# A two-layer recurrence on one core: a loop body of four slots, and two copies by ScalarE

## The reference

```python
xW = jnp.einsum('ntd,dh->nth', x, Wx) + b
def step(h_prev, xw_t):
    h_next = jnp.tanh(h_prev @ Wh + xw_t)
    return (h_next, h_next)
x = x + _L0_cond_ref(x, cond_1024, L0_cond_Wx, L0_cond_Wh, L0_cond_b)
x = x + _L1_cond_ref(x, cond_1024, L1_cond_Wx, L1_cond_Wh, L1_cond_b)
```

## Time and profile before

| what | before |
|---|---|
| median of three runs | 2059.51 us |
| profiled execution, first to last instruction | 2057.6 us |
| TensorE matmul / weight load busy | 2044.6 / 1863.8 us |
| VectorE busy | 1746.3 us |
| ScalarE busy | 1280.9 us |
| GpSimd busy | 444.9 us |
| one slot in the steady part | 1.98 us |

### The profile page before, as it was taken

How to read it: one execution, slowest core, us unless ns; L and a number is a source line. 1 busy time by engine, 2 the same in 40 slices (tenths; PEclk the granted TensorE clock), 3 DMA queues, 4 the chain that set the end, 5 groups by cost and what they waited for, 6 DMA issues and landing times.

```text
span 2057.6 us, 219078 instructions
## 1 busy us (share of the span) xinstructions
PE 2044.6 (99%) x98388; PEld 1863.8 (91%) x98388; DVE 1746.3 (85%) x10221; ACT 1280.9 (62%) x6660; POOL 444.9 (22%) x2054
## 2 busy tenths in 40 slices
PE   8999999999999999999999999999999999999999
PEld 6999999999999999999999999999999999999997
DVE  5888888888888888888888888888888888888887
ACT  4666666666666666666666666666666666666665
POOL 3222222222222222222222222222222222222221
DMA  3000000000000000000000000000000000000000
GB/s 108 25 26 25 26 25 26 25 26 25 27 24 27 24 28 24 28 24 28 24 27 24 27 24 27 24 27 24 28 23 28 23 27 24 27 24 27 24 27 15
DMA packets 111960, 56.33 MB, mean 27 GB/s; under 512 B 12432, under 2 KB 111008, under 8 KB 111520
## 3 DMA queue, kind: packets, MB, share of 16 engines
q1 hardware_dynamic: 111168, 53.53, 8.8%
q10 hardware_dynamic: 576, 1.18, 0.2%
q0 software_dynamic: 32, 0.02, 0.0%
HBM read 37.90 MB, written 16.78 MB: 27 GB/s over the span
## 4 chain that ended last, share of the span: by engine, by line
PE 99%; DMA 1%; issue 0%; DVE 0%; ACT 0%; SPq 0%; ACTq 0%
PE ps_rec L270 44%; PE ps_rec L287 33%; PE ps_xw L247 22%; DMA wx<-wx_in 0%; DMA wh<-wh_in 0%; PE ps_rec L339 0%; DVE zt L463 0%; ACT h L387 0%; SPq L223 0%; ACTq L421 0%; ACTq L420 0%; DVE z L472 0%; DVE x_out L503 0%; SPq L222 0%
## 5 line engine op out<-in xcount | busy, mean ns | idle before, releaser
L270 PE MATMUL ps_rec<-wh,h 128*32 128x128 f32 x33024 | 1261.2, 273 | 3.3 <-ACT h L387 2.8
L387 ACT ACTIVATE h<-z 128x24 f32<-128x24 f32 x4066 | 654.7, 208 | 666.4 <-DVE z L472 625.0
L287 PE MATMUL ps_rec<-wh_part,h 128*32 128x128 bf16 x48792 | 1036.9, 219 | 1.5 <-issue 1.5
L270 PEld LDWEIGHTS ps_rec<-wh,h 128*32 128x32 f32 x33024 | 880.0, 109 | 30.1 <-ACT h L387 6.7
L287 PEld LDWEIGHTS ps_rec<-wh_part,h 128*32 128x32 bf16 x48792 | 724.0, 96 | 151.1 <-issue 1.8
L205 POOL TENSOR_TENSOR h<-h 128x16 f32<-128x16 f32 x2032 | 430.6, 212 | 1589.9 <-DVE h L205 1589.9
L472 DVE TENSOR_REDUCE z<-zt 128x24 f32<-128x72 f32 x4066 | 664.5, 205 | 69.7 <-DVE zt L463 0.6
L376 ACT ACTIVATE ps_rec<-ps_xw,mask 128x128 f32<-128x128 f32 x2048 | 664.2, 324 | 77.9 <-PE ps_xw L247 77.9
L463 DVE STREAM_TRANSPOSE zt<-ps_rec 128x128 f32<-128x128 f32 (+1 forms) x2063 | 649.8, 316 | 18.7 <-PE ps_rec L270 12.7
L205 DVE TENSOR_TENSOR h<-h 128x16 f32<-128x16 f32 x2034 | 356.0, 175 | 209.2 <-ACT h L387 0.2
L247 PE MATMUL ps_xw<-wx,x_pe 128*32 128x128 f32 x8248 | 404.6, 273 | 2.0 <-issue 1.1
(11 more groups left out here) (20 smaller groups left out, 16.5 us busy)
## 6 DMA issues: line engine op xcount, KB each, us to landing
x_pe<-x_t SPq DMA_DIRECT2D x256, 64.0 KB, 2.0
x_dve<-x_t SPq DMA_DIRECT2D x256, 64.0 KB, 1.9
out_t<-x_out SPq DMA_DIRECT2D x256, 64.0 KB, 1.5
wh<-wh_in SPq DMA_DIRECT2D x1, 1024.0 KB, 5.7
wx<-wx_in SPq DMA_DIRECT2D x1, 1024.0 KB, 8.3
wx<-wx_in ACTq DMA_DIRECT2D x1, 512.0 KB, 5.2
wx<-wx_in SPq DMA_DIRECT2D x1, 512.0 KB, 5.0
wh<-wh_in SPq DMA_DIRECT2D x1, 512.0 KB, 7.2
```

Source lines behind the costliest of these rows:

```text
L270: mm = pe.matmul(rows(ps_rec[l][n % 2], g), h_step(l, n - 1)[:, k, :], wh[l][:, k, g * P:(g + 1) * P], start=False, stop=k == KC - 1 and n ...
L287: mm = pe.matmul(rows(ps_rec[l][n % 2], g), h_bits(l, n - 1)[:, k, :], wh_part[l][:, i, at:at + P], start=False, stop=k == KB[l] - 1 and i ...
L387: act.activation(h_of(l, n)[:, tiles, :], src[:, tiles, :], ACT.Tanh).then_inc(h_count(l, n)[0], 1)
```

## The change

- `RING` becomes 4: h is kept for four steps instead of eight, and TensorE's loop body has four slots (254 turns instead of 127). LAG stays 7. Counts that were lowered every four slots are lowered every two (`PAIR`).
- `PIECES` (24 + 8 columns) goes; every step uses `HALVES`. The transpose becomes two of 64 columns, the reduces and tanhs two of 16. `recur_whole` of two tiles waits once, for the second half. `rec_done` becomes one semaphore for each layer.
- `ps_xw` of layer 1 is one bank, and layer 0 uses only its first one after the second group. ScalarE copies each finished projection into SBUF (`copy`, buffers `xw`), and `begin` reads there.
- Layer 1's operand is `xm_pe`, one buffer, copied from `x_mid` by ScalarE (`pass_xm`), for each group. TensorE waits for `xm_done` at the first tile of each group of layer 1.
- `x_pe` has one buffer after the first two groups; SP waits for one group more before it loads.
- ScalarE's order in a slot is new, as is the place of `begin` of layer 1 (one step ahead, before its tanh).
- `make_parts`, `PLAN`, `LAST`, `SPLITS`, `LATE`, `POOL_MAKES` and `DVE_MAKES` have values here with which they give the instructions of before in the same order.

```diff
@@ -23,20 +23,28 @@
-RING = 8
-HALF = 4 * (P + B)
-LAG = RING - 1
+RING = 4
+PAIR = 2
+LAG = 7
...
-PARTED = RING
-FIRST = 1
-AFTER = T // RING
+PARTED = 8
...
-PIECES = (slice(0, KC - 1), slice(KC - 1, KC))
+SIDE = P // 2
+
+
 HALVES = (slice(0, KC // 2), slice(KC // 2, KC))
...
+PLAN = (((0, BOTH), (1, BOTH)), ((0, BOTH), (1, BOTH)))
+LAST = ((1,), (1,))
+SPLITS = (1, 1)
...
-        h = [sb(f"h{l}", [P, 2 * HALF + B]) for l in LAYERS]
+        h = [sb(f"h{l}", [P, RING * (P + B) + B]) for l in LAYERS]
...
-        ps_xw = [[psum(f"ps_xw{l}_{i}") for i in range(2)] for l in LAYERS]
+        xm_pe = sb("xm_pe", [P, GRP])
+        xw = [[sb(f"xw{l}_{i}", [P, P]) for i in range(2 - l)] for l in LAYERS]
+
+        ps_xw = [[psum(f"ps_xw{l}_{i}") for i in range(2 - l)] for l in LAYERS]
...
-            return LAG - LAG % S4 <= s < T + LAG if l else 0 <= s < T
+            return LAG - LAG % PAIR <= s < T + LAG if l else 0 <= s < T
...
             s = n + LAG * l
-            steps = [(m, t) for t in range(s - s % S4, s + 1) for m in LAYERS if counted(m, t)]
-            return h_done[s // S4 % 2], 2 * steps.index((l, s)) + piece + 1
+            steps = [(m, t) for t in range(s - s % PAIR, s + 1) for m in LAYERS if counted(m, t)]
+            return h_done[s // PAIR % 2], 2 * steps.index((l, s)) + piece + 1
...
+        def piece_count(n, piece):
+
+            return 2 * n + piece + 1
...
+        def split_count(l, n, piece):
 
             s = n + LAG * l
-            return split_done[l][s // S4 % 2], s % S4 + 1
+            return split_done[l][s // PAIR % 2], SPLITS[l] * (s % PAIR) + piece + 1
...
-            return w // 4 * HALF + w % 4 * P + (32 if w % 4 == 3 else 0), B * ((n + 1) % 4)
+            return w * P + (32 if w == RING - 1 else 0), B * ((n + 1) % S4)
...
+            def load_x_pe(c):
+                sp.dma_start(x_pe[0][:, :], x[:, c, :]).then_inc(x_pe_loaded, DMA)
...
             for c in range(1, NG + 4):
                 if 3 <= c + 1 < NG:
-                    sp.wait_ge(proj_done[0], c)
-                    load(x_pe, x_pe_loaded, c + 1)
+                    sp.wait_ge(proj_done[0], c + 1)
+                    load_x_pe(c + 1)
...
             def project(l, c, k):
 
-                src = (x_mid if l else x_pe)[c % 2][:, k * ROWS:(k + 1) * ROWS]
+                src = xm_pe if l else x_pe[c == 1]
                 for g in range(QG):
-                    mm = pe.matmul(rows(ps_xw[l][c % 2], g), src, wx[l][:, k, g * P:(g + 1) * P], start=False,
-                                   stop=False, skip_group_check=True, tile_position=(0, 32 * g))
+                    mm = pe.matmul(rows(ps_xw[l][l == 0 and c == 1], g), src[:, k * ROWS:(k + 1) * ROWS],
+                                   wx[l][:, k, g * P:(g + 1) * P], start=False, stop=False, skip_group_check=True,
+                                   tile_position=(0, 32 * g))
...
-                if l or n:
-                    pe.wait_ge(*h_count(l, n - 1, 0))
...
-                    pe.wait_ge(*h_count(l, n - 1, 0))
-                else:
+                if (l, n) == (0, 0):
                     pe.wait_ge(s_hinit, 2)
                     pe.wait_ge(begun[0], 1)
-                for k in range(in_parts(l, n), KC):
+                tiles = range(in_parts(l, n), KC)
+                for k in tiles:
                     if (l, n) == (0, 0):
-                        pe.wait_ge(s_wh0[k // 2], DMA)
-                    elif k == pieces(l, n - 1)[1].start:
-                        pe.wait_ge(*h_count(l, n - 1))
+                        if k % 2 == 0:
+                            pe.wait_ge(s_wh0[k // 2], DMA)
+                    elif k % 2 == 0 or k == tiles[0]:
+                        pe.wait_ge(*h_count(l, n - 1, k // 2))
                     for g in range(QG):
                         mm = pe.matmul(rows(ps_rec[l][n % 2], g), h_step(l, n - 1)[:, k, :],
...
-                    mm.then_inc(rec_done, 1)
+                    mm.then_inc(rec_done[l], 2)
 
...
 
 
                 if not in_parts(l, n):
                     return
-                pe.wait_ge(*split_count(l, n - 1))
-                for k in range(KB[l]):
+                waited = -1
+                for at, (k, sides) in enumerate(PLAN[l]):
+                    if k // 2 > waited:
+                        waited = k // 2
+                        pe.wait_ge(*split_count(l, n - 1, waited))
+                    cols = slice(sides.start * SIDE, sides.stop * SIDE)
                     for i in range(PARTS):
                         for g in range(QG):
...
+                    if at in LAST[l]:
+                        mm.then_inc(rec_done[l], 2 // len(LAST[l]))
 
             def projection(s, half):
...
-                        pe.wait_ge(seed0_done[c % 2], 1)
+                        if c == 2:
+                            pe.wait_ge(s_seed, 4)
+                        else:
+                            pe.wait_ge(seed0_done, 1)
                     if k == 0 and (l, c) == (1, 0):
                         pe.wait_ge(s_wx1, DMA)
-                    if k == 0 and l == 1 and c in (0, NG - 1):
-                        pe.wait_ge(mid_done, c + 1)
+                    if k == 0 and l == 1:
+                        pe.wait_ge(xm_done, 1)
                     project(l, c, k)
 
...
+            for s in range(PARTED):
+                slot(s)
             pe.wait_ge(s_wpart[0], PARTS * KB[0])
-            with pe.Fori(0, AFTER - FIRST, 1):
-                turn(FIRST)
-            turn(AFTER)
+            with pe.Fori(0, (T - PARTED) // RING, 1):
+                for s in range(PARTED, PARTED + RING):
+                    slot(s)
+            for s in range(T, T + LAG):
+                slot(s)
...
 
-                return act.activation(ps_xw[l][c % 2][:, 0:P], bias[l][:, :], ACT.Copy)
+                return act.activation(ps_xw[l][l == 0 and c == 1][:, 0:P], bias[l][:, :], ACT.Copy)
+
+            def direct(l, c):
+
+                return l == 0 and c < 2
+
+            def copy(l, c):
+
+                act.wait_ge(proj_done[l], c + 1)
+                if c > 1 - l:
+                    act.wait_ge(begun[l], S4 * (c - 1 + l))
+                act.activation(xw[l][c % (2 - l)][:, :], ps_xw[l][0][:, 0:P], ACT.Copy).then_inc(copied[l], 1)
+
+            def copy_count(l, c):
+
+                return c + 1 if l else c - 1
 
             def begin(l, n):
 
                 c, t = n // S4, n % S4
                 if t == 0:
-                    act.wait_ge(proj_done[l], c + 1)
-                act.activation(ps_rec[l][n % 2][:, 0:P], ps_xw[l][c % 2][:, 0:P], ACT.Copy,
+                    if direct(l, c):
+                        act.wait_ge(proj_done[l], c + 1)
+                    else:
+                        act.wait_ge(copied[l], copy_count(l, c))
+                src = ps_xw[l][c][:, 0:P] if direct(l, c) else xw[l][c % (2 - l)][:, :]
+                act.activation(ps_rec[l][n % 2][:, 0:P], src, ACT.Copy,
                                scale=mask[:, 32 * t:32 * t + 1]).then_inc(begun[l], 1)
 
             def tanh(l, n):
-                for i, tiles in enumerate(pieces(l, n)):
+                for i, tiles in enumerate(HALVES):
                     if is_whole(l, n):
-                        act.wait_ge(zt_done[l], zt_count(l, n, i))
+                        act.wait_ge(zt_done[l], piece_count(n, i))
                         src = rows_of_h(l, n)
                     else:
                         act.wait_ge(z_done[l], z_count(l, n, i))
                         src = z[l][n % 2][:, :].rearrange("p (k b) -> p k b", k=KC)
                     act.activation(h_of(l, n)[:, tiles, :], src[:, tiles, :], ACT.Tanh).then_inc(h_count(l, n)[0], 1)
 
+            def pass_xm(c):
+
+                act.wait_ge(mid_done, c + 1)
+                if c:
+                    act.wait_ge(proj_done[1], c)
+                act.activation(xm_pe[:, :], x_mid[c % 2][:, :], ACT.Copy).then_inc(xm_done, 1)
+
             def slot(s):
 
 
-                last = [(l, s - 1 - LAG * l) for l in LAYERS if counted(l, s - 1)]
-                for l in LAYERS:
-                    if (n := number(l, s)) is not None:
-                        tanh(l, n)
-                    if l == 1 and s % S4 == 0 and s:
-                        done, count = h_count(*last[-1])
-                        act.sem_inc(done, -count)
-                    if l == 0 and s % S4 == 1 and 2 <= (c := (s + 7) // S4) < NG:
-                        act.wait_ge(x_pe_loaded[c % 2], DMA * (c // 2))
-                    if (n := number(l, s + 2)) is not None and n >= 2:
-                        begin(l, n)
-                    elif l == 1 and s + 2 == LAG + 1:
-                        begin(l, 0)
-                        begin(l, 1)
-                        act.wait_ge(begun[1], 2)
-                    if l == 1 and s < LAG and counted(l, s):
-                        act.wait_ge(*h_count(0, s))
-                        act.sem_inc(h_done[s // S4 % 2], 2)
```

(102 more changed lines are left out.)

52 lines of the change are left out of this document (24 added, 28 removed).

## The result

The changed kernel takes 2156.48 us (median of 4 runs, 2155.72 to 2157.35) against 2059.28 us before: slower, ratio 1.0473 (95% interval 1.0458 to 1.0488). The forecast was 2153.5 us, range 2130 to 2205. The profiled execution's span went from 2057.6 to 2155.6 us, 98.0 more.

The account below looks back on a forecast made before the run. TensorE's streaming was taken as the bound. Span 2057.6 plus 94.0 (254 stalls of 0.37 us, other steps at no cost) gave 2151.6, plus 1.9 from span to median made 2153.5 us; range 2130 to 2205.

Parts of the forecast that it names:

- What bounds the kernel: TensorE's own streaming time sets the half slot of 0.99 us; no wait delays it, and any stop is never caught up.
- The operand's copy: ScalarE's xm_pe copy behind layer 0's tanhs stalls TensorE before layer 1's projection: 254 x 0.37 = 94.0 us.
- Halves at no cost: Halved transpose, reduces and tanhs: whole product's slack 0.09 to 0.05 us, split product's 0.02 to 0.11; nothing lost.
- Copies of the projections at no cost: ScalarE's added projection copies, 0.28 to 0.32 us each, fit its idle time with 0.12 us of cover; cost 0.
- x_pe with one buffer and SP's queue: The single x_pe buffer's load lands at 1007.95, before ScalarE asks at 1009.7; transfers queued on SP wanted later; cost 0.
- Loop ends at 1 us: TensorE's four-slot loop body adds 127 loop ends, at most 0.01 us each, 1 us.
- The late halves: Rival: halves reach the whole product late, 0.035 us each half slot, 71 us on top, about 2225; chance 0.10.
- the hidden copy: Rival: ScalarE's xm_pe copy runs early enough, or TensorE has other work first; 2059 to 2061 us; chance 0.04.
- the faster ring: Rival: transpose, reduce, tanh, subtract set the 0.99 us; halves shorten it by 0.09; about 1970 us; chance 0.03.
- The dear loop ends: Rival: 127 more of TensorE's loop ends, some 108 ns each, all exposed, add 14 us, 2167; chance 0.03.

Follow-up runs that it names:

- experiments 4: Changed kernel with one more same-size copy, into a buffer nobody reads, ahead of ScalarE's copy into xm_pe: 2208.24 us in one run.
- experiment 5: Changed kernel with the copy into xm_pe cut in two, 32 columns first and then 96, each with its own wait: 2136.46 us in one run.
- experiment 3: Kernel before with only the halves added (two 64-column transposes, pieces of 16 and 16 columns): 2060.16 us, ratio 1.0007.
- experiment 1: Changed kernel with ScalarE's copy into xm_pe issued at the end of slot 4r-1 instead of behind layer 0's tanhs in slot 4r: 2058.51 us, ratio 0.9997.
- experiment 2: Kernel of experiment 1 with TensorE's loop body written out for eight slots instead of four: 2061.04 us.
- experiment 7: Kernel of experiment 1 with the old pieces again (one 128x128 transpose, reduces and tanhs of 24 and 8 columns): 2057.21 us, ratio 0.9991.

## Why the prediction was right

**What bounds the kernel.** Confirmed by all runs: whatever was moved, a half slot without a wait stayed at 0.99 us, and where TensorE's stops were lengthened or shortened (experiments 4 and 5) the time followed in full.

**The operand's copy** carried the whole sum. Term by term, with T = 1010.43 in the changed kernel's chain above:

| term | forecast | measured |
|---|---|---|
| start of the copy | T+0.78 | T+0.78 (1011.21) |
| its duration | 0.30 (0.275 to 0.324) | 0.293, group mean |
| copy's end to the matmul | 0.05 | 0.06 |
| projection starts | T+1.13 | T+1.13 (1011.56) |
| wanted at | T+0.76 | T+0.77 (1010.86 + 0.34) |
| stall | 0.37 | 0.362 (median), and 0.024 at the restart |
| groups | 254 | 253 waits in the view |

The row of the copy, and that of the reduces which the forecast had between two neighbours (0.205 us):

```profile
L452 ACT ACTIVATE xm_pe<-x_mid 128x128 f32<-128x128 f32 x256 | 75.0, 293 | 0.3 <-issue 0.2
...
L550 DVE TENSOR_REDUCE z<-zt 128x16 f32<-128x48 f32 x4066 | 650.2, 199 | 0.9
```

The copy's price is that of the page "ScalarE: Activation LUTs" of the Trainium skill (What ACT_TABLE_LOAD costs): 186 ns and 0.833 ns a column, an estimate of 0.293. The 32 and 96 column copies of experiment 5 took 213 and 267 ns, where it gives 213 and 266. By rows alone the middle of two neighbours was 7 ns off. Those 7 ns are 1.8 us over 254 groups; the 2.5 us that the prediction gives for them come from rounding the stall to 0.36.

**What was missing in the sum** is the 0.02 us of the restart: 254 x 0.02 = 5 us. The forecast let the matmuls go on at their old distance once the load was there. In fact the whole product starts 0.242 us after the projection and not 0.218. Usually a load runs ahead of its matmul, and after a stop both start together (1011.55 and 1011.56); that this costs the 0.02 is my reading, not something a run tested. The stall itself was 0.008 us shorter than forecast, and together a group cost 0.386 us.

That 254 x 0.386 = 98.0 us is just the difference between the spans is in part luck, because small terms that the forecast had not cancel. By the starts of the split products the 253 stalls come to 98.8 us, since six of them were 0.09 to 0.27 us longer than the rest. Small stops outside them add 1.3 us to what the kernel before has. The first pass over TensorE's loop body costs 3.1 us instead of 5.7, and the loop starts 0.6 us later.

**The other steps.** Halves at no cost: right, with both slacks (experiment 3). Copies of the projections at no cost: right, as experiment 1 has them all. x_pe with one buffer and SP's queue: right; no wait for a transfer of x_pe appears in the steady part. Loop ends at 1 us: right that they are not paid each turn, wrong in sign for the whole, since the shorter body saved 2.5 us (experiment 2), which the small stops took back (3.0 against 0.5 us).

**The rivals.** The late halves fell with experiments 1 and 3, the hidden copy with the result itself, the faster ring with experiment 3 and with half slots that stayed at 0.99 us. The dear loop ends fell with experiment 2: the 108 ns of a compare and branch that "Advanced Engine Details and Errata" of the Trainium skill (Control Flow Timing) gives are not seen at any loop end here. That matmuls queued ahead cover them may be, but was not tested.

## What to carry to other kernels

When an operand gets an extra copy on another engine, ask where the copy stands in that engine's program, not how long it takes: behind an operation that it doesn't need, it inherits that operation's lateness, and on a bound engine the consumer pays for it each time. The same instruction issued where its input becomes ready, 0.7 us earlier, cost nothing here, and that decided over 97 us. Work out the moment the result is ready and the moment it is wanted, both from one common event in the trace; the difference times the count is the change.

## What the runs showed of the hardware that was not expected

**Restart after a stop.** TensorE loses 0.024 us more than the wait: from projection to whole product 0.242 for 0.218 us, the same in the median of the changed kernel and of experiments 4 and 5.

**Small stops of VectorE and ScalarE.** In the kernel of experiment 1, half slots of 1.04 to 1.15 us come at distances such as 35.7 us, which hold 256 recorded VectorE instructions, or 17.9 us with 129. One of them, in VectorE's timeline:

```profile
384.96 0.38 DVE L541 STREAM_TRANSPOSE zt<-ps_rec 128x64 f32<-128x64 f32 x2
385.44 0.33 DVE L550 TENSOR_REDUCE z<-zt 128x16 f32<-128x48 f32 x2
```

The reduce starts 0.48 us after the transpose; usually it is 0.31 (in the changed kernel 1010.43 and 1010.74):

```profile
1010.43 0.38 DVE L541 STREAM_TRANSPOSE zt<-ps_rec 128x64 f32<-128x64 f32 x2
1010.74 0.32 DVE L550 TENSOR_REDUCE z<-zt 128x16 f32<-128x48 f32 x2
```

The page "Advanced Engine Details and Errata" of the Trainium skill (ISA Cache) has instruction memory in lines of 16 KB, 256 instructions. The distance fits; that these stops are refills was not tried, for instance by making VectorE's program a loop. Not every such distance has a long half slot. How much of a stop reaches TensorE goes by the slack: with the whole product's 0.05 us they cost 3.0 us, with the old pieces' 0.09 (experiment 7) 1.5.

Four of the 30 begin on ScalarE, like this one, where the copy follows the tanhs after 0.58 us instead of 0.28:

```profile
55.28 0.35 ACT L445 ACTIVATE h<-z 128x16 f32<-128x16 f32 x2 [0.18 <-DVE z L550]
55.86 0.28 ACT L419 ACTIVATE xw<-ps_xw 128x128 f32<-128x128 f32 x1 [0.23 <-issue]
```

**The first pass over a loop body** cost TensorE 2.5 us with four slots (1.9 in a second profile) and 5.5 with eight; later passes show no such stop. The cause is open in the same way.
